# Attention and FFN on one core: direct end of the last half, early copies of two GELU pieces, and FFN2 thirds put between scores and V products

## The reference, cut to what matters

```python
xn = _layernorm(x)
# attention, per batch and head: q = k = v = xn
w = einsum('bhqd,bhkd->bhqk', q, k) / sqrt(hd)
w = softmax(where(causal, w, min))
attn = einsum('bhqk,bhkd->bhqd', w, v)
# feed-forward; m1, m2 are products of eight rows of xn each
h = einsum('bsd,hd->bsh', xn, W1) + scale * einsum('bsd,bhd->bsh', xn, m1) + b1
h = gelu(h, approximate=False)
ffn = einsum('bsh,oh->bso', h, W2) + scale * einsum('bsh,boh->bso', h, m2) + b2
return x + attn + ffn
```

## Time and profile before

| | |
|---|---|
| median of 3 runs | 926.56 us (925.12 to 927.49) |
| the profiled execution | 927.0 us, span 925.3 us |
| PE matmul busy | 853.4 us (92%), 7040 instructions |
| ACT busy | 684.5 us (74%) |
| DVE busy | 625.6 us (68%) |
| POOL busy | 201.3 us (22%) |
| chain that ended last, by engine | PE 59%, DVE 21%, ACT 12%, DMA 2% |
| granted TensorE clock, mean | 0.993 |

### The profile page before, as it was taken

How to read it: one execution, slowest core, us unless ns; L and a number is a source line. 1 busy time by engine, 2 the same in 40 slices (tenths; PEclk the granted TensorE clock), 3 DMA queues, 4 the chain that set the end, 5 groups by cost and what they waited for, 6 DMA issues and landing times.

```text
span 925.3 us, 17547 instructions
## 1 busy us (share of the span) xinstructions
PE 853.4 (92%) x7040; PEld 483.1 (52%) x7040; DVE 625.6 (68%) x1260; ACT 684.5 (74%) x737; POOL 201.3 (22%) x264
## 2 busy tenths in 40 slices
PE   1689999999999999999999999999999999999994
PEld 1255555556465564645556564555646556464652
DVE  7876677758777596676877677774877659671422
ACT  0558787787878878787887878778787877878782
POOL 1202123121312213132231212322031221212120
PEclk9999999999999999999999999999999999999997
DMA  4846436462463635455363733646256454513103
GB/s 132 318 140 185 126 100 192 141 179 75 121 199 120 171 98 171 125 175 185 103 189 84 210 106 104 207 124 177 74 149 171 146 146 124 151 30 114 25 6 103
DMA packets 212145, 127.18 MB, mean 137 GB/s; under 512 B 139168, under 2 KB 180320, under 8 KB 211040
## 3 DMA queue, kind: packets, MB, share of 16 engines
q1 hardware_dynamic: 212064, 126.06, 46.6%
HBM read 84.02 MB, written 42.01 MB: 136 GB/s over the span
## 4 chain that ended last, share of the span: by engine, by line
PE 59%; DVE 21%; ACT 12%; issue 3%; DMA 2%; POOL 2%; SPq 1%; DVEq 0%; ACTq 0%
PE o_ps L455 20%; PE work L470 14%; PE work L483 13%; PE scores L435 11%; ACT probs L391 9%; DVE w_lo L596 3%; DVE xn L557 3%; DVE stats L538 2%; POOL probs L383 2%; DVE xt_lo L596 2%; DVE w_hi L593 2%; DVE xt_hi L593 2%; ACT L401 1%; ACT gelu L401 1%; DVE acc L661 1%
## 5 line engine op out<-in xcount | busy, mean ns | idle before, releaser
L391 ACT ACTIVATE probs<-scores 128x1024 f32<-128x1024 f32 x576 | 555.7, 1024 | 143.7 <-PE scores L435 143.5
L383 POOL TENSOR_SCALAR_AFFINE_SELECT probs<-probs 128x512 f32<-128x512 f32 x256 | 198.7, 794 | 704.5 <-ACT probs L391 704.5
L455 PE MATMUL o_ps<-probs,v_ones 128*32 128x512 f32 (+3 forms) x3072 | 283.0, 492 | 6.7 <-POOL probs L383 4.9
L435 PE MATMUL scores<-q_stack,k_stack 64*128 64x512 f16 (+3 forms) x1536 | 186.3, 330 | 20.7 <-ACT probs L391 12.2
L455 PEld LDWEIGHTS o_ps<-probs,v_ones 128*32 128x32 f32 x3072 | 83.0, 109 | 139.5 <-issue 109.6
L483 PE MATMUL work<-w_hi,g_hi 128*128 128x256 f32 x512 | 155.8, 304 | 0.0
L483 PE MATMUL work<-w_lo,g_hi 128*128 128x256 f32 x512 | 146.0, 285 | 0.0
L483 PE MATMUL work<-w_hi,g_lo 128*128 128x256 f32 x512 | 145.7, 285 | 0.0
L401 ACT ACTIVATE gelu<-work,b_sb 128x512 f32<-128x512 f32 x128 | 86.5, 688 | 78.3 <-PE work L470 72.0
L435 PEld LDWEIGHTS scores<-q_stack,k_stack 64*128 64x128 f16 x1536 | 52.0, 94 | 153.8 <-ACT probs L391 107.7
L483 PEld LDWEIGHTS work<-w_hi,g_hi 128*128 128x128 f32 x512 | 96.8, 189 | 44.3 <-issue 41.3
(11 more groups left out here) (41 smaller groups left out, 548.7 us busy)
## 6 DMA issues: line engine op xcount, KB each, us to landing
q_stack<-q_dram SPq DMA_DIRECT2D x32, 512.0 KB, 4.9
k_stack<-k_dram SPq DMA_DIRECT2D x64, 256.0 KB, 5.0
q_dram<-xt_pair SPq DMA_DIRECT2D x30, 512.0 KB, 5.2
xn<-x SPq DMA_DIRECT2D x16, 512.0 KB, 5.4
w<-w1t SPq DMA_DIRECT2D x8, 1024.0 KB, 8.8
even<-even_dram SPq DMA_DIRECT2D x8, 1024.0 KB, 5.4
xt_w<-w2t SPq DMA_DIRECT2D x8, 1024.0 KB, 5.8
acc<-x SPq DMA_DIRECT2D x8, 1024.0 KB, 6.9
```

Source lines behind the costliest of these rows:

```text
L383: pool.affine_select(out=blk, in_=blk, compare_op=ALU.is_ge, fill=0.0, base=0, pattern=[[0, GH], [1, P]], channel_multiplier=-1).then_inc( ...
L391: act.activation(probs[:, slot % RING, 2 * half:2 * half + 2, :].rearrange("p h q -> p (h q)"), scores[:, half, :], ACT.Exp, scale=EXP_SCA ...
L435: last = pe.matmul(scores[:, half, h * BANK + at:h * BANK + at + n], k_stack[rows, g % 2, half, kb * P:(kb + 1) * P], q_stack[rows, g % 2, ...
L455: last = pe.matmul(o_ps[VW * j:VW * (j + 1), half, q0 % BANK:q0 % BANK + n], v_ones[:, kb, GH * g + j, :], probs[:, slot % RING, j, at:at ...
```

## The change

Four parts. (1) For the last half of the last batch the path over DRAM goes for the last group: DVE copies `o_ps` to `o_sb`, PE transposes it in four blocks into `scores`, and DVE divides and adds from there into `acc`. The other three groups of that half are loaded and added early, at pair 15. (2) The first two pieces of each half of `ffn1` are copied out of `work` by DVE, which frees the bank; ACT then computes the GELU in place in `gelu`. (3) At pair 10 `split_pair` of the second channel tile stands behind `split_gelu` instead of before it. (4) In pairs 14 to 16 PE goes scores, V product, 4 passes of FFN2, scores, V product, 4 passes of FFN2.

```diff
 BETWEEN = {
     2: [("ffn2", 0, 0, 0, 12, 0)],
     11: [("ffn2", 1, 0, 0, 12, 0)],
+    14: [("ffn2", 1, 2, 0, 4, 0)],
+    15: [("ffn2", 1, 2, 8, 12, 0)],
+    16: [("ffn2", 1, 2, 16, 20, 0)],
 }
+SINGLE = (14, 15, 16)
 BEHIND = {
...
-    14: [("ffn2", 1, 2, 0, 8, 0)],
-    15: [("ffn2", 1, 2, 8, 16, 0)],
-    16: [("ffn2", 1, 2, 16, 24, 0)],
+    14: [("ffn2", 1, 2, 4, 8, 0)],
+    15: [("ffn2", 1, 2, 12, 16, 0)],
+    16: [("ffn2", 1, 2, 20, 24, 0)],
...
+LAST = (B - 1, 1)
+LAST_ADD_O = (17, 15)
+ORDER_O = {(b, half): 2 * b + (half if b < B - 1 else 1 - half) + 1 for b in range(B) for half in range(2)}
+EARLY = 2
...
             def load_o(b, half):
-                sp.wait_ge(o_stored[half], 16 * GH * GROUPS * (b + 1))
...
+                last = (b, half) == LAST
+                cols = D - GH * HD if last else D
+                sp.wait_ge(o_stored[half], 16 * GH * (GROUPS * (b + 1) - last))
...
                 store_o(b, 2, 1)
+                if b == B - 1:
+                    load_o(b, 1)
                 store_o(b, 3, 0)
...
-            store_o(B - 1, GROUPS - 1, 1)
-            load_o(B - 1, 1)
             store_acc(B - 1, 1)
...
             def gelus(b, c):
                 for m in range(MT):
...
+                    if m < EARLY:
+                        act.wait_ge(work_free[bank], had + 1)
+                        act.activation(gelu[:, m % 2, :], gelu[:, m % 2, :], ACT.Gelu,
+                                       bias=b1_sb[:, m:m + 1]).then_inc(gelu_early, 1)
+                        continue
...
                         times_v(slot)
-                        times_v(slot + 1)
+                        if p not in SINGLE:
+                            times_v(slot + 1)
                     for what, of, *arg in work_of(BETWEEN, b, p):
                         ffn2(of, *arg)
                     if slot + 3 < ALL:
                         scores_of(slot + 3)
+                    if p in SINGLE:
+                        times_v(slot + 1)
+                    if b == B:
+                        pe.wait_ge(o_evac[1], GROUPS * B)
+                        for t in range(TB):
+                            last = pe.transpose(scores[:, 0, P * t:P * (t + 1)], o_sb[:, P * t:P * (t + 1)], ident[:, :])
+                        last.then_inc(last_ready, 1)
...
+            def evac_last():
+                dve.wait_ge(pv_done, ALL)
+                dve.tensor_copy(o_sb[:, :], o_ps[:, 1, :]).then_inc(o_evac[1], 1)
+
+            def add_last():
+                dve.wait_ge(last_ready, 1)
+                o_t = scores[:, 0, 0:BANK].rearrange("p (t h c) -> p t h c", t=TB, h=GH)
+                sums = rden[:, :, :].rearrange("p (t h) c -> p t h c", t=TB)
+                link(dve.reciprocal(sums, o_t[:, :, :, HD:HD + 1]))
+                norm = o_norm[:, 1, :, :].rearrange("p (t h) c -> p t h c", t=TB)
+                dve.wait_ge(o_stored[1], 16 * GH * (GROUPS * B - 1))
+                link(dve.tensor_tensor(norm, o_t[:, :, :, 0:HD], sums.broadcast_to([P, TB, GH, HD]), ALU.mult))
+                part = acc[:, (B - 1) % 2, TB:NT, D - GH * HD:D].rearrange("p t (h c) -> p t h c", h=GH)
+                link(dve.tensor_tensor(part, part, norm, ALU.add))
...
             def split_gelu(b, c):
+                for m in range(EARLY):
+                    bank, _, end = USE["ffn1", b, c, m]
+                    dve.wait_ge(work_ready, end + 1)
+                    dve.tensor_copy(gelu[:, m % 2, :], work[:, bank, :]).then_inc(work_free[bank], 1)
                 for m in range(MT):
-                    evacuated("ffn1", b, c, m)
+                    if m < EARLY:
+                        dve.wait_ge(gelu_early, EARLY * (2 * b + c) + m + 1)
+                    else:
+                        evacuated("ffn1", b, c, m)
                     split(g_hi[:, m, :], g_lo[:, m, :], gelu[:, m % 2, :], g_split)
...
                             evac_xt(of, *arg)
-                            if arg[0] % 2:
-                                split_pair(of, arg[0] // 2)
+                            if arg[0] == 1:
+                                split_pair(of, 0)
+                    if more and ("xn", XT_USES - 1) in BEHIND[p]:
+                        split_pair(b + 1, 1)
```

More of the change, by code:

```diff
@@ L215, in attention_ffn @@
         work_free = [sem("work_free0"), sem("work_free1")]
-        g_split, m2_added = sem("g_split"), sem("m2_added")
+        g_split, m2_added, gelu_early = sem("g_split"), sem("m2_added"), sem("gelu_early")
         w1_ready, w2_ready = sem("w1_ready"), sem("w2_ready")
         xn_ready, pair_ready, xt_split, v_ready = sem("xn_ready"), sem("pair_ready"), sem("xt_split"), sem("v_ready")
-        acc_done = sem("acc_done")
+        o_added, last_ready, last_done = sem("o_added"), sem("last_ready"), sem("last_done")
         chain = sem("chain")
@@ L236, in store_acc @@
                 blocks = slice(TB * half, TB * (half + 1))
-                sp.wait_ge(acc_done, 2 * b + half + 1)
+                if (b, half) == LAST:
+                    sp.wait_ge(last_done, 1)
+                else:
+                    sp.wait_ge(o_added, ORDER_O[b, half])
                 sp.dma_start(out[b, :, :].rearrange("(t p) d -> p t d", p=P)[:, blocks, :], acc[:, b % 2, blocks, :])\
@@ L281, in load_o @@
             def load_o(b, half):
-                sp.wait_ge(o_stored[half], 16 * GH * GROUPS * (b + 1))
-                if b or half:
-                    sp.wait_ge(acc_done, 2 * b + half)
-                sp.dma_start(o_tok[:, :, :], o_dram[b, BANK * half:BANK * (half + 1), :]
+                last = (b, half) == LAST
+                cols = D - GH * HD if last else D
+                sp.wait_ge(o_stored[half], 16 * GH * (GROUPS * (b + 1) - last))
+                if ORDER_O[b, half] > 1:
+                    sp.wait_ge(o_added, ORDER_O[b, half] - 1)
+                sp.dma_start(o_tok[:, :, 0:cols], o_dram[b, BANK * half:BANK * (half + 1), 0:cols]
                              .rearrange("(t p) d -> p t d", p=P)).then_inc(o_in, 16)
@@ L395, in gelus @@
                 for m in range(MT):
-                    bank, _, end = USE["ffn1", b, c, m]
+                    bank, had, end = USE["ffn1", b, c, m]
                     done = MT * (2 * b + c) + m
+                    if m < EARLY:
[3 more added lines that the diff above has]
+                        continue
                     act.wait_ge(work_ready, end + 1)
-                    if done >= 2:
-                        act.wait_ge(g_split, done - 1)
+                    act.wait_ge(g_split, done - 1)
                     act.activation(gelu[:, m % 2, :], work[:, bank, :], ACT.Gelu,
@@ L658, in add_o @@
             def add_o(b, half):
-                dve.wait_ge(o_in, 16 * (2 * b + half + 1))
-                part = acc[:, b % 2, TB * half:TB * (half + 1), :]
-                dve.tensor_tensor(part, part, o_tok[:, :, :], ALU.add).then_inc(acc_done, 1)
+                cols = D - GH * HD if (b, half) == LAST else D
+                dve.wait_ge(o_in, 16 * ORDER_O[b, half])
+                part = acc[:, b % 2, TB * half:TB * (half + 1), 0:cols]
+                dve.tensor_tensor(part, part, o_tok[:, :, 0:cols], ALU.add).then_inc(o_added, 1)
+                if (b, half) == LAST:
+                    dve.wait_ge(o_added, ORDER_O[b, half])
+            def evac_last():
[11 more added lines that the diff above has]
+                link(dve.tensor_tensor(part, part, norm, ALU.add))
             def add_ffn(b, c, tb):
@@ L707, in _ @@
                     for s in (slot, slot + 1):
-                        if s < ALL and s % NS in HALF_DONE:
+                        if s == ALL - 1:
+                            evac_last()
+                        elif s < ALL and s % NS in HALF_DONE:
                             evac_o(s)
+                    if b == B:
+                        add_last()
                     if b == 0 and p == 2:
@@ L719, in _ @@
                             evac_xt(of, *arg)
-                            if arg[0] % 2:
-                                split_pair(of, arg[0] // 2)
+                            if arg[0] == 1:
+                                split_pair(of, 0)
+                    if more and ("xn", XT_USES - 1) in BEHIND[p]:
+                        split_pair(b + 1, 1)
                     for half in range(2):
-                        at, later = ADD_O[half]
+                        at, later = ADD_O[half] if b < B - 1 or b == B - 1 and p < LAST_ADD_O[1] else (LAST_ADD_O[half], 0)
                         if p == at and 0 <= b - later < B:
@@ L753, in _ @@
                             add_m2(b + 1)
-            add_o(B - 1, 1)
+            dve.sem_inc(last_done, 1)
 def kernel(**inputs):
```

## The result

The changed kernel takes 936.8 us (median of 4 runs, 936.0 to 938.3) against 925.8; the ratio is 1.0108, 95% interval 1.0093 to 1.0123. It is slower by 11, where 926.8 and a range up to 932.5 were forecast. The profiled execution takes 936.0, its span is 934.2, 8.9 more than before.

What follows compares the result with a forecast made beforehand. PE, busy 92%, was taken as the bound, so its idle places count. The profiled 927.0 - 8.3 (end) + 0.3 (copies) + 8.2 (order and split_pair) = 927.2, lying 0.4 above the median, gave 926.8; range 920.5 to 932.5.

Steps and rivals of the forecast that it cites:

- The end: After PE's last pass the kernel waits 8.03 for the way over DRAM; the direct path was to save 8.3.
- Early copies: First two ffn1 pieces: -3.4 and -0.9 at c = 1, +2.8 at c = 0, +1.8 in batch 0; sum +0.3.
- Slots of 2.21 and a gain of 1.06 a batch without the stall: Pairs 14 to 16: PE needs 2.20 a slot, ACT's loop allows 2.21; without other waits, 1.06 less a batch.
- The stall: Pair 14, FFN2 block (1,2): its bank is free only after DVE adds block (1,1); +1.17 a batch, +8.2 in seven.
- push: The moved split_pair delays DVE's add of block (1,1): 0 to 1.4 possible, taken as 0.75.
- The part about the masks: POOL's masks slow a DVE split by 0.87; DVE shifted by 1 us meets them otherwise, so some delay returns.
- the rule of the exclusive pair of ports: DVE and POOL block each other on shared SBUF ports; masks cost the same anywhere, nothing returns, push 0.97, sum 928.3.
- the clock falls in each new stall: Rival: if PE's 2.2 idle in pair 14 halves the clock for 3 us, +10.5 in all, 937.3; chance 9%.
- The price of one fall: PE's clock halved for 3 us after a stall in pair 14 was to cost 1.5 more each.

Runs made afterwards that it cites:

- e6: The kernel before with only the direct end of the last half (no early copies, old split_pair place, old order); 917.9 us, ratio 0.9896.
- e1: The changed kernel with the old order in pairs 14 to 16, all else as changed; 924.5 us, ratio 0.998.
- e7: e4 with early copies only at c = 1; 908.2 us, ratio 0.9791.
- e4: The changed kernel with FFN2 block (1,2) in the other bank of work; 913.5 us, ratio 0.986.
- e2: The kernel before with only the new order in pairs 14 to 16; 929.6 us, ratio 1.003.
- e3: The changed kernel with split_pair of the second tile ahead of split_gelu again; 933.6 us, ratio 1.008.
- e10: e3 with one more DVE addition of 128x256, result unused, behind split_m1; 943.8 us, ratio 1.0184.
- e9: The changed kernel with two more DVE additions of 128x512, results unused, behind split_m1 in pair 12; 950.7 us, ratio 1.0253.
- e5: The changed kernel with 16 useless PE matmuls ahead of the waiting FFN2 block in pair 14, batches 0 to 6; 929.5 us, ratio 1.0022.
- e8: e7 with the new order in pairs 5 to 7 too; 914.0 us, ratio 0.9859.

## Why the prediction was wrong

- **The end** (-8.3): right. Alone it is -8.2 by the profiled spans, about 8.7 between runs of like clock (e6).
- **Early copies** (+0.3): right at c = 0, 1.30 - 0.88 = +0.42 a batch (forecast 0.40). At c = 1 the wait is gone, and what comes back is 0.4 by e1 (forecast 0.48). In batch 0 the way from `ffn1` to `ffn1` grew by 0.8, where 1.8 was put. e7 against e4, where the copies at c = 0 are taken away, gives 3.6 by the profiled spans: 3.0 in batches 1 to 7, 0.4 in batch 0 and 0.4 ahead of it. By the medians it is 5.3; the profiled execution of e4 was the fastest of its four by 1.5.
- **Slots of 2.21 and a gain of 1.06 a batch without the stall**: right, 2.2 and 1.03 in e4.
- **The stall**: right. PE was to stand from 1.53 behind the scores of pair 14 until DVE's add, with a push of 0.75; the add came 3.38 behind those scores where it had been 2.54 (+0.84), and the stall is 2.21. The part about the masks held half: w_lo fell from 3.37 to 2.81, but xt_lo rose from 2.50 to 2.93 and the additions of `add_m1` from 3.26 to 3.63. By the rule of the exclusive pair of ports (the Trainium skill, SBUF — State Buffer, section "SBUF: two separate sides"), read as the prediction reads it, the push was 0.97. That and my own 0.75 stand either side of the 0.84 measured; the trace does not decide between them. What the stall and the early copy at c = 1 cost together, without the clock, is 0.86 a batch where 1.17 - 0.48 = 0.69 was forecast.
- **The clock**: this is the step that failed. The sum had no term for it, and the rival "the clock falls in each new stall" got 9%, with the argument that idles of 0.9 left the clock at full and only 4.05 was seen to drop it. Nothing in the trace past the start of the kernel lay between 0.9 and 4.05, the new stall of 2.2 lay right there, and I gave the unknown to the side that suited the sum. The runs: no fall in fourteen stalls of 1.4 (e2, e3), three and five of seven at 2.2 (e10 and the changed kernel), seven of seven at 3.4 (e9), and none where the stall of 2.2 was filled (e5). The price of one fall was right, 1.5. With 5 x 1.5 the sum is 934.7 in place of 927.2 for the profiled execution of 936.0. Of the remaining 1.3 the stall's price makes 7 x 0.17. The other differences nearly cancel: batch 0 costs 1.0 less than forecast, and the stretch ahead of its `ffn1` is 0.8 longer (41.57 against 40.80), which no term of the forecast has.

The page named for that rival would not have settled it. The Trainium skill (TensorE: Matmul & The Clock Gate, section "Why this matters for your kernels") wants no idle gaps of PE between bursts of matmuls, but only above a length that this stall of 2.2 does not reach. Taken with that limit it speaks for a clock that holds; the runs show eight falls in fourteen stalls of 2.2, and the measurement decides. The range was too narrow as well: an unknown with ends 0 and +10.5 should have kept both ends.

## What to carry to other kernels

When an order on PE is changed, look for the first instruction of every moved block and ask which buffer it takes and who frees it: here the thirds moved ahead by one block, and a bank that had always been free in time was not. A second buffer that stood idle made 937 into 913. And price a new idle stretch of PE twice, as its length and as what follows if the clock drops: where the trace has no idle of that length, both ends belong in the range.

## What the runs showed of the hardware

- The same stall of 2.2 us drops the granted clock in some batches and not in others: five of seven in one kernel, three of seven in another, in a program whose batches are otherwise alike. At 1.4 it never fell, at 3.4 always. Batch 0 has a like pair, PE's idle for the third piece of `ffn1` in e2 and in e8:

```profile
51.37 0.50 PE L474 MATMUL work<-xt_hi,w_hi 128*128 128x512 f32 x1 [2.92 <-ACT gelu L405]
```

```profile
51.58 0.80 PE L494 MATMUL work<-xt_hi,w_hi 128*128 128x512 f32 x1 [2.89 <-ACT gelu L425]
```

  From 51.50 to 54.50 the granted clock is 1.00 in e2 and 0.50 in e8. What decides between two stalls of equal length was not tested and stays open.
- Keeping PE busy with useless matmuls in seven stalls of 2.2 saved 7.3 us, and no fall of the clock was left behind any of them (e5).
- A DVE addition of 0.41 us shifted the work behind it by 0.8 (e10 against e3), because the next multiplication fell beside two masks on POOL: it took 0.81 instead of 0.42. The same holds for subtractions of 128x512, four of which took 3.37 beside masks and 2.50 without.
